# A second fold in the search for the 64 largest scores of an attention phase

## What is computed

```python
q = (x @ Wq).reshape(b, n, H, DH).transpose(0, 2, 1, 3)     # H = 16 heads of DH = 64, n = 512 queries
k = concatenate([mem_k, k], axis=2)                         # M = 16 memory keys ahead of the 512
dots = einsum('bhid,bhjd->bhij', q, k) * SCALE
dots = einsum('bhij,hk->bkij', dots, pre_proj)              # heads are mixed
dots = where(causal, mask_value, dots)
kth = top_k(dots, TOPK)[0][..., -1:]                        # TOPK = 64: the 64th largest score of each row
dots = where(dots < kth, mask_value, dots)
attn = softmax(dots, axis=-1)
out = einsum('bhij,bhjd->bhid', attn, v)
```

## Time and profile before

| | us |
|---|---|
| median of three runs | 5477.86 |
| the three runs | 5485.43, 5477.67, 5477.86 |
| span of the profiled execution | 5483.6 |
| of it, ahead of the selecting attention's slots | 2342 |
| the slots of the selecting attention | 1320 |
| behind them | 1821 |

### The profile page before, as it was taken

One profiled execution on the slowest core, in us unless ns is written; L12 is line 12 of the kernel. 1 busy time (PEld: TensorE's weight loads), 2 busy tenths in 40 slices (PEclk: granted clock), 3 DMA queues, 4 the chain that ended last, 5 costly groups with the idle time before them and its releaser, 6 DMA issues. The chain is left out here.

```text
span 5483.6 us, 135449 instructions
## 1 busy us (share of the span) xinstructions
PE 4765.3 (87%) x51638; PEld 3038.8 (55%) x51638; DVE 4170.6 (76%) x8694; ACT 3355.0 (61%) x7201; POOL 2738.0 (50%) x3646
## 2 busy tenths in 40 slices
PE   4775999999999999677767768667999999999997
PEld 1222666666666666434444343344666666666665
DVE  5897777777777777389898999966777777777774
ACT  2432677777777777344445444435777777777775
POOL 1221666666666666223232332325666666666663
PEclk7898999999999999888888888868999999999998
DMA  0000222222222222100000000002232223222221
GB/s 18 0 0 19 70 74 65 73 71 69 68 71 73 64 75 63 32 1 2 2 2 2 2 2 2 2 1 73 65 81 62 73 67 78 64 74 67 77 64 36
DMA packets 162489, 247.16 MB, mean 45 GB/s; under 512 B 36228, under 2 KB 56640, under 8 KB 161734
## 3 DMA queue, kind: packets, MB, share of 16 engines
q1 hardware_dynamic: 161862, 238.65, 16.7%
HBM read 36.15 MB, written 1.05 MB: 7 GB/s over the span
## 5 line engine op out<-in xcount | busy, mean ns | idle before, releaser
L940 POOL TENSOR_TENSOR f_rope<-f_rope,f_t 128x1024 f32<-128x1024 f32 x384 | 906.3, 2360 | 520.7 <-DVE f_t L854 520.7
L953 POOL TENSOR_TENSOR f_rope<-f_rope,f_rn 128x1024 f32<-128x1024 f32 x384 | 731.2, 1904 | 56.8 <-POOL f_rn L932 2.6
L490 PE MATMUL psum<-f_wqkv,f_xs 128*128 128x512 f32 x1536 | 731.7, 599 | 22.4 <-DVE f_t L854 22.4
L859 DVE TENSOR_REDUCE f_ss<-f_sq 128x16 f32<-128x1024 f32 x384 | 459.5, 1197 | 336.8 <-ACT f_sq L721 334.6
L1806 POOL TENSOR_SCALAR tk_scores<-tk_scores,tk_m 128x408 f32<-128x408 f32 (+28 forms) x232 | 240.3, 1036 | 826.2 <-DVE tk_m L1766 628.2
L1766 DVE MAX8 tk_m<-tk_work 128x8 f32<-128x204 f32 (+38 forms) x1856 | 620.7, 380 | 39.5 <-ACT tk_neg_top L1654 37.3
L1777 DVE MATCH_REPLACE8 tk_work<-tk_m,tk_work 128x204 f32<-128x204 f32 (+51 forms) x1624 | 581.1, 365 | 0.0
L684 ACT ACTIVATE f_kT<-psum 64x512 f32<-64x512 f32 (+1 forms) x960 | 485.5, 525 | 85.9 <-PE psum L481 76.4
L721 ACT ACTIVATE f_sq<-psum 128x1024 f32<-128x1024 f32 x384 | 393.5, 1025 | 217.3 <-PE psum L490 216.7
L854 DVE TENSOR_TENSOR f_t<-psum,f_rot 128x1024 f32<-128x1024 f32 x384 | 466.1, 1214 | 0.0
L850 DVE TENSOR_TENSOR f_rope<-psum,f_rot 128x1024 f32<-128x1024 f32 x384 | 465.2, 1212 | 0.0
(11 more groups left out here) (235 smaller groups left out, 9319.3 us busy)
## 6 DMA issues: line engine op xcount, KB each, us to landing
f_v<-f_v_tok SPq DMA_DIRECT2D x1152, 128.0 KB, 2.4
f_v<-f_v_tok SPq DMA_DIRECT2D x768, 64.0 KB, 2.0
f_wqkv<-in_Wqkv SPq DMA_DIRECT2D x36, 512.0 KB, 4.0
f_wo<-in_Wo SPq DMA_DIRECT2D x12, 512.0 KB, 4.1
f_w<-in_W SPq DMA_DIRECT2D x12, 341.0 KB, 3.2
f_w<-in_W SPq DMA_DIRECT2D x24, 64.0 KB
tk_wkv<-in_Wkv SPq DMA_DIRECT2D x1, 1024.0 KB
out<-y_tok SPq DMA_DIRECT2D x4, 256.0 KB, 2.5
```

Source lines behind the costliest of these rows:

```text
L490: last = pe.matmul(psum[:, n, :], xs[:, j % 2, :], wqkv[:, INNER * which + 512 * n:INNER * which + 512 * (n + 1)], start=True, stop=True)
L859: dve.tensor_reduce(ss[:, H * half:H * (half + 1)], sq[:, half, :, :], AX_X, ALU.add).then_inc(s[f"{name}_ss"], 1)
L940: pool.tensor_tensor(part, part, t2[:, half, :, :], ALU.add).then_inc(s[f"{name}_added"], 1)
L953: pool.tensor_tensor(part, part, rn[:, H * half:H * (half + 1)].unsqueeze(2).to_broadcast([P, H, DH]), ALU.mult).then_inc(s[f"{name}_norme ...
```

## The change

For pairs whose first unit has 240 columns or more, a second fold is put ahead of round 4. By then the 32 largest of the first half of `tk_work` are overwritten. `refold` writes to a new tile `tk_again` the maximum (columns 0 to h) and the minimum (columns h to n) of the two halves of what is left. Of the 32 largest values that are left at least 16 lie in the first half, so rounds 4 and 5 read h columns of `tk_again`, and rounds 6 and 7 its n columns. Of the search order nothing else is changed, and pairs of fewer columns are as before. Pairs with 240 columns or more are those of n = 248 and 264 in the third tile and all 16 of the first two tiles: 18 pairs in a batch, 72 in all, 144 units.

```diff
+    def folds_twice(p):
+        return extent(2 * p)[0] >= 240
...
+        again = sb("again", [P, 2, MEM + N])
...
+                def refold(p):
+
+                    for j in range(2):
+                        n, h = extent(2 * p + j)[0], half(2 * p + j)
+                        src, dst = work[:, p % 2, j, :], again[:, j, :]
+                        dve.wait_ge(s["removed"], 1 + count["removed"] - 1 + j)
+                        dve.tensor_tensor(dst[:, 0:h], src[:, 0:h], src[:, h:n], ALU.max).then_inc(s["refolded"], 1)
+                        dve.tensor_tensor(dst[:, h:n], src[:, 0:h], src[:, h:n], ALU.min).then_inc(s["refolded"], 1)
+                    count["refolded"] += 4
...
                     rounds = ROUNDS if selects(2 * p) else 1
+                    twice = rounds > 1 and folds_twice(p)
                     for r in range(rounds):
                         if rounds == 1:
                             src = [scores[:, p % 3, j, 0:cols[j]] for j in range(2)]
+                        elif twice and r >= ROUNDS // 2:
+                            src = [again[:, j, 0:half(2 * p + j) if r < 3 * ROUNDS // 4 else cols[j]] for j in range(2)]
                         else:
                             src = [work[:, parity, j, 0:half(2 * p + j) if r < ROUNDS // 2 else cols[j]] for j in range(2)]
+                        if twice and r == ROUNDS // 2:
+                            refold(p)
                         for j in range(2):
-                            if r:
+                            if twice and r == ROUNDS // 2:
+                                dve.wait_ge(s["refolded"], 1 + count["refolded"] - 2 + 2 * j)
+                            elif r:
                                 dve.wait_ge(s["removed"], 1 + count["removed"] - 1 + j)
```

More of the change, by code:

```diff
@@ L1380, in topk_phase @@
         s = names(ctx, "tk", nc, "w_in", "mem_turned", "mem_copied", "scaled", "chosen", "zeroed", "mixer", "side_full", "side_evac",
-                  "raw_full", "raw_copied", "mixed", "copied", "folded", "top", "m8", "removed", "kth", "kept", "neg_top", "e_done", "p_done", "turned", "turn_evac",
+                  "raw_full", "raw_copied", "mixed", "copied", "folded", "refolded", "top", "m8", "removed", "kth", "kept", "neg_top", "e_done", "p_done", "turned", "turn_evac",
                   "pv_full", "rden", "o_done", "ot_full", "ot_evac", "y_done", "added")
@@ L1723, in _ @@
             def _(dve):
-                count = {"m8": 0, "removed": 0}
+                count = {"m8": 0, "removed": 0, "refolded": 0}
                 def recip(blk):
```

## The result

The changed kernel takes 5443.69 us (median of 4 runs, 5438.05 to 5450.28), the kernel before 5481.65 us beside it (4 runs, 5477.67 to 5487.98). The ratio is 0.9931, with an interval of 0.9916 to 0.9946 (29.6 to 46.0 us): 38.0 us faster, where 38.5 were forecast, and inside the range. Runs of the kernel before spread from 5467 to 5496 us there, and the experiments show what goes with part of that spread.

The account below looks back on a forecast made before the run. The prediction took DVE to bound the long pairs: 116.7 us removed less 77.6 added gives 39.1 net, less 0.6 lost in the first pair is 38.5, so 5477.9 - 38.5 = 5439.4 us; range 5433 to 5458.

Parts of the forecast that it names:

- DVE sets the pace in the long pairs: Selecting attention: DVE has no idle time in the long pairs, while no other engine passes 73% there.
- The sum: DVE, changed pairs: 116.7 us removed, 77.6 us added (1.044 ns a column, 0.067 us an instruction), net 39.1 us saved.
- What hides: First pair's 0.6 us is lost as DVE waits for ACT ahead of pair 1; 38.5 us reach the end.
- Rival 2: Refold: each added instruction takes its full duration, 0.09 us more each, 26 us in all, 5465.4 us; chance 6%.
- Rival 3: Refold: waits on the directly preceding DVE instruction cost 0.21 us each, 76 us in all, 5515 us; chance 3%.
- Rival 1: PE and ACT take over the pace: 5455.6 us without second and third tiles' gains, 5477.9 without any; chance 8%.
- Rival 4: Refold reads two tensors while POOL selects: a meeting costs POOL about 0.5 us and changes the forecast by nothing.
- the one of pair 74: Thinnest lead behind the start: ACT finishes 4.5 us before DVE starts pair 74; 3.8 us remain after the change.

Follow-up runs that it names:

- no_refold: The changed kernel without the 288 added refold instructions, leaving out part of the computation; 5376.13 us, ratio 0.9813 to the kernel before.
- third_fold: The changed kernel with a third fold ahead of round 6, four more instructions in each changed pair; 5461.57 us, ratio 0.9977 to the kernel before.
- first_tile: The changed kernel with the refold restricted to pairs of 400 or more columns; 5455.07 us, ratio 0.9968 to the kernel before.
- after_again: The changed kernel run once more, unaltered, as base for the other runs; 5446.0 us, ratio 0.9944 to the kernel before.
- pool_twice: The changed kernel with POOL's multiplication of the second unit done twice in changed pairs; 5483.82 us, ratio 1.0012 to the kernel before.
- quarter: The changed kernel with the larger half folded once more for rounds 0 and 1 in 61 pairs; 5452.61 us, ratio 0.9958 to the kernel before.
- quarter_late: quarter with the next pair's fold and quartering moved from behind round 6 to behind round 7; 5506.63 us, ratio 1.0059 to the kernel before.
- direct_waits: The changed kernel with the refold's units in the other order, so two waits fall on the instruction directly before; 5461.59 us, ratio 0.9971 to the kernel before.

## Why the prediction was right, and where it only seemed so

- **DVE sets the pace in the long pairs.** Right: it is busy in all of them, and no_refold shows that this holds for a saving of 117 us too.
- **The sum.** Right by term: 1.044 ns a column by the tiles (4.4 and 3.5 us against 4.5 and 3.5), 0.067 us fixed by third_fold (1.6 and 2.2 against 1.6 and 2.1), and additivity by first_tile.
- **What hides.** Right: 0.6 us is lost ahead of pair 1, and nowhere else does DVE wait anew. One reading was off without effect: of the waits before, 0.49 us (at 2675.5) stands ahead of the second batch's first pair, which has 408 columns, and not in pairs of 24 to 184. It lies ahead of that pair's refold and touches none of its saving.
- **Rival 2, full durations.** Wrong as forecast: starts 0.28 us apart.
- **Rival 3, waits on the instruction before.** The mechanism is real, at 0.12 us each here and not 0.21. The row that I took the price from the earlier trace rows was of another kind of instruction on 512 columns. The refold as written pays none of it.
- **Rival 1, PE and ACT.** It is not in the long pairs, as the leads said. But in the short pairs, where DVE waits for ACT, the time goes with PE's granted clock, and moves the total by 10 us and more. The prediction allowed "a few" us for runs to differ, which is too little: after_again's 31 us and the first result's 38 are the same change.
- **Rival 4, POOL in the way.** The step that failed is "a meeting costs POOL about 0.5 us ... It changes the forecast by nothing". It took from one meeting who pays, and that meeting was of another kind: POOL's instruction was the comparison, with one tensor in, and it began in the same instant as DVE's fold. Where POOL's multiplication is first, DVE pays: 0.39 to 0.73 us a pair in pool_twice, 38 us in all against after_again, more than the change brings in that group. I also read the Trainium skill (GPSIMD Engine Reference, Key points) as borne out with POOL as the payer; the runs show the contention it names on both sides. The forecast held because in the changed kernel POOL is done 0.43 us before the refold begins (2435.79 against 2436.22), which on this point was luck. It follows, too, that a semaphore wait is not the only thing that ties an instruction to another engine: the held ones wait for no semaphore of POOL's. The trace of the kernel before gave this margin, and the prediction did not work it out. At the same place there, POOL and then DVE's round 4, ahead of which the refold goes:

```profile
2440.16 1.23 POOL L1808 TENSOR_TENSOR tk_e<-tk_scores,tk_e 128x496 f32<-128x496 f32 x1
```

```profile
2441.80 1.27 DVE L1766 MAX8 tk_m<-tk_work 128x8 f32<-128x504 f32 x2
```

POOL ends at 2441.39, 0.41 us before 2441.80. This should have been a term with a lead of its own, like the one of pair 74.

What stays open: why the clock in the short pairs is low in one batch and high in the next, and if a faster long stretch makes it so. It was not tried, since it would need many profiles of one kernel. Open as well is who pays when POOL's multiplication begins in the middle of a run of DVE's two-input instructions (below).

## What to carry to other kernels

Price a saving on the engine that is never idle by the distance from start to start, and it comes true to a tenth of a microsecond, as long as the added instructions meet nothing. For each two-input DVE instruction added or moved, look at what POOL does at that time: the distance to POOL's nearest instruction is a lead like any other, and 0.4 us of it carried this whole gain. Judge a gain of half a per cent from stretches of the trace that hold the changed work, and only then from totals.

## What the runs showed of the hardware

- A DVE TENSOR_TENSOR issued while a POOL TENSOR_TENSOR runs can be held until that one ends: 0.90 for 0.41 us (quarter), 1.20 for 0.41 (pool_twice), 1.29 for 0.28 (quarter_late). Where POOL's began before DVE's run of such instructions, the first of the run was held in 150 of 166 meetings in the thirteen traces, and in 14 of the other 16 POOL's had less than 0.2 us left.
- Where POOL's multiplication begins in the middle of a run of DVE's, either engine can pay: DVE's next instruction was held in 54 such meetings (1.25 for 0.38 us at 2366.53 in direct_waits), and in 47 it was not, and POOL's was the longer one. In the changed kernel the one of 528 columns falls beside the refold of the next, shorter pair and takes 1.69 us where 520 columns take 1.30, and where it took 1.30 in the kernel before. POOL's groups by form of the changed kernel (busy us, mean ns), then the one of before:

```profile
L1829 POOL TENSOR_TENSOR tk_e<-tk_scores,tk_e 128x528 f32<-128x528 f32 x4 | 6.8, 1689 | 0.3
...
L1829 POOL TENSOR_TENSOR tk_e<-tk_scores,tk_e 128x520 f32<-128x520 f32 x4 | 5.2, 1300 | 0.3
```

```profile
L1808 POOL TENSOR_TENSOR tk_e<-tk_scores,tk_e 128x528 f32<-128x528 f32 x4 | 5.2, 1300 | 0.3
```

- POOL's one-input comparison holds DVE's TENSOR_TENSOR near its start (0.62 for 0.41 us, 0.32 us behind that start), but not later on. In the thirteen traces 145 were held, by 0.4 us at most; all had begun 0.14 to 0.46 us behind the comparison's start, though not all that began there were held, and of the 511 that began over 0.5 us behind it none was. In the changed kernel, first POOL, then DVE, which begins 0.68 us behind the comparison's start and takes its usual 0.37:

```profile
2365.20 1.32 POOL L1827 TENSOR_SCALAR tk_scores<-tk_scores,tk_m 128x416 f32<-128x416 f32 x1
```

```profile
2365.88 0.37 DVE L1755 TENSOR_TENSOR tk_again<-tk_work 128x212 f32<-128x212 f32 x1
```

- No MAX8 or MATCH_REPLACE8, with one tensor in, was held beside POOL: of some 20,000 in the thirteen traces that began while an instruction of POOL's ran, none is over 0.14 us longer than 1.044 ns a column plus 0.15 us.
- A wait on the instruction directly before costs DVE 0.12 us at 252 and 256 columns, with one instruction in between nothing.
- The stretch with the same 652 matmuls of the short pairs took 63.9 us at a granted clock of 0.89 and 75.5 us at 0.71 within one execution (direct_waits).
